# Graph layer of a GNN and mixture-of-experts block: two bins of nodes to a PSUM bank, one look a turn, row lists by fourteens

## What is computed

```
y = layernorm(x)
w_full = einsum('rb,bdo->rdo', w_comp, weight)          # 16 relations out of 8 bases
msg = einsum('nd,rdo->rno', y, w_full)[etypes, src] * edge_weight
x = x + relu(segment_sum(msg, dst) + h_bias + y @ loop_weight)
x = x + expert_layer(layernorm(x))
```

## Time and profile before

| | us |
|---|---|
| median of three runs (3833.6 to 3851.45) | 3844.34 |
| profiled execution, its own time | 3843.4 |
| its span, first to last instruction | 3841.7 |
| graph layer: first gather issued | 215.1 |
| last gather issued | 3008.9 |
| last multiplication of a turn starts | 3101.3 |

### The profile page before, as it was taken

One profiled execution on the slowest core, in us unless ns is written; L12 is line 12 of the kernel. 1 busy time (PEld: TensorE's weight loads), 2 busy tenths in 40 slices (PEclk: granted clock), 3 DMA queues, 4 the chain that ended last, 5 costly groups with the idle time before them and its releaser, 6 DMA issues. The chain is left out here.

```text
span 3841.7 us, 44188 instructions
## 1 busy us (share of the span) xinstructions
PE 2433.4 (63%) x11555; PEld 1907.4 (50%) x11556; DVE 942.2 (25%) x2185; ACT 682.4 (18%) x1839; POOL 1874.2 (49%) x2177
## 2 busy tenths in 40 slices
PE   3544454554655655666666666767767756999976
PEld 1422332433543443454454455555556536888865
DVE  4611111121102112121111111112112246333336
ACT  0510000000011111111111122212222211222234
POOL 0466666566546546555545445345544201444433
PEclk9866676776877877888878877888788878999998
DMA  3442333233223223222222223222222242112135
GB/s 117 146 135 85 88 92 88 75 92 97 73 75 90 78 74 94 77 82 80 78 76 78 78 76 90 66 68 78 83 83 64 52 144 93 63 63 63 61 123 189
DMA packets 144937, 337.27 MB, mean 88 GB/s; under 512 B 36515, under 2 KB 52163, under 8 KB 144740
## 3 DMA queue, kind: packets, MB, share of 16 engines
q0 software_dynamic: 89392, 245.59, 21.9%
q1 hardware_dynamic: 34239, 51.42, 3.9%
q10 hardware_dynamic: 21252, 39.56, 3.0%
HBM read 289.22 MB, written 50.42 MB: 88 GB/s over the span
## 5 line engine op out<-in xcount | busy, mean ns | idle before, releaser
L1176 PE MATMUL psW<-rows,S 128*128 x3920 | 1192.7, 459 | 878.2 <-issue 590.9
L994 POOL DMA_INDIRECT rows<-feat,idx x1568 | 1489.9, 950 | 479.6 <-issue 460.5
L1176 PEld LDWEIGHTS psW<-rows,S 128*128 128x128 f32 x3920 | 850.2, 228 | 1215.1 <-issue 1095.4
L1076 DVE TENSOR_TENSOR S<-psHere,coefS 128x896 f32<-128x896 f32 x280 | 303.8, 1091 | 2227.8 <-PE psW L1176 1244.3
L1235 ACT COPY z<-psW 128x256 f32<-128x256 f32 x392 | 145.6, 371 | 2064.1 <-PE psW L1176 1080.2
L977 POOL COPY idx<-srcT 128x7 int32 (+1 forms) x224 | 43.6, 195 | 783.9 <-PE psW L1176 616.4
L1139 PE MATMUL psG<-wb,zT 128*128 128x256 f32 (+1 forms) x1600 | 357.9, 382 | 0.0
L1139 PEld LDWEIGHTS psG<-wb,zT 128*128 128x128 f32 (+1 forms) x1600 | 304.1, 190 | 47.5 <-issue 1.0
L1126 PE MATMUL psZ<-ident,z 128*128 128x128 f32 x784 | 152.5, 352 | 197.1 <-ACT z L1235 91.2
L1126 PEld LDWEIGHTS psZ<-ident,z 128*128 128x128 f32 x784 | 114.8, 180 | 236.0 <-issue 184.5
L1562 PE MATMUL psH<-xT,w1x 128*128 128x128 f32 x1840 | 228.3, 278 | 0.2 <-DVE w1x L1604 0.2
(11 more groups left out here) (254 smaller groups left out, 1449.6 us busy)
## 6 DMA issues: line engine op xcount, KB each, us to landing
rows<-feat,idx POOLq DMA_INDIRECT x1568
g<-expert_rows SPq DMA_DIRECT2D x24, 512.0 KB, 5.8
w1s<-in_L_ffn_w SPq DMA_DIRECT2D x8, 1024.0 KB, 10.7
w2s<-in_L_ffn_w SPq DMA_DIRECT2D x16, 512.0 KB, 10.9
featT<-fT ACTq DMA_DIRECT2D x25, 256.0 KB, 2.2
fts<-featT ACTq DMA_DIRECT2D x25, 256.0 KB
feat<-yt SPq DMA_DIRECT2D x24, 256.0 KB, 2.2
h<-in_x ACTq DMA_DIRECT2D x24, 256.0 KB
```

Of the source, the lines that this page charges most:

```text
L994: e.indirect_dma_start(rows[:, at * H:(at + 1) * H], None, d.feat, bass.IndirectOffsetOnAxis(ap=idx[:, q * GB + u:q * GB + u + 1], axis=0) ...
L1076: e.tensor_tensor(S[h][:, :].rearrange("p (s b n) -> p s b n", s=U, b=B), both[:, h * U:(h + 1) * U, :].unsqueeze(2).to_broadcast([P, U, B ...
L1176: e.matmul(psW[:, bass.ds(bank[u], H)], S[h][:, u * ZC:(u + 1) * ZC], rows[:, bass.ds(slot[u], H)], start=False, stop=True, skip_group_che ...
```

## The change

- Two bins share a bank: steps address eight half banks. ScalarE waits for the second bin of a pair, copies both to `z` with one instruction of 512 columns, and clears both with one. `wend`, the counts of `z_done` and of `cleared` go by pairs. Eight bins are in flight in place of four.
- TensorE takes a turn as a whole: one look for a tile's end, one wait for a clear place (of the turn's last bin), one for landed rows (of its last block), one for `S`, then seven multiplications. The table has 20 numbers for a turn in place of 24.
- POOL's lists are of `GB` = 14 blocks, and SyncE counts landed rows by `QB` = 7. The ring stays at 56 blocks.
- The cuts of the loop move (82, 70, 66, 62 turns), and `expand` works out the smaller tables.

```diff
-CTL = 24
+CTL = 20
 RB = 56
-GB = 7
-QB = 4
+GB = 14
+QB = 7
...
-CTL_PART = (78, 62, 70, 70)
+CTL_PART = (82, 70, 66, 62)
...
             for k in range(NB):
-                e.matmul(psW[:, k * BANK:k * BANK + H], zero[:, 0:P], zero[:, :], start=True, stop=True).then_inc(s_clear, 1)
+                e.matmul(psW[:, k * BANK:k * BANK + H], zero[:, 0:P], zero[:, :], start=True, stop=True)
+                e.matmul(psW[:, k * BANK + H:(k + 1) * BANK], zero[:, 0:P], zero[:, :], start=False, stop=True, skip_group_check=True).then_inc(s_clear, 1)
...
                         e.load(regs, ctl[part_of][:, bass.ds(i * 2 + h, 1), :])
-                        for k, (u0, n) in enumerate(PART):
-                            tile1 = e.snap(regs[AT_TILE + k], min_val=1, max_val=NT2)
-                            with e.If(e.snap(regs[AT_ENDED + k], min_val=0, max_val=1)):
-                                tile_product(tile1, TW)
...
-                            e.wait_ge(s_clear, clear)
-                            e.wait_ge(s_in, come)
-                            if k == 0:
-                                e.wait_ge(s_S, i * 2 + (first + h + 1))
-                            for u in range(u0, u0 + n):
...
+                        tile1 = e.snap(regs[AT_TILE], min_val=1, max_val=NT2)
+                        with e.If(e.snap(regs[AT_ENDED], min_val=0, max_val=1)):
+                            tile_product(tile1, TW)
...
+                        e.wait_ge(s_clear, clear)
+                        e.wait_ge(s_in, come)
+                        e.wait_ge(s_S, i * 2 + (first + h + 1))
+                        for u in range(U):
...
-                for k in range(nw):
-                    if later(t) and k == nw // 2:
+                for k in range(nw // 2):
+                    if later(t) and k == nw // 4:
                         e.wait_ge(s_tile, t)
                         columns_in(t)
                     e.wait_ge(s_P, regs[k])
-                    at = k % NB * BANK
-                    e.copy(z[:, k * H:(k + 1) * H], psW[:, at:at + H]).then_inc(s_z, 1)
-                    e.wait_ge(s_z, t * TW + k + 1)
-                    e.copy(psW[:, at:at + H], zero[:, :]).then_inc(s_clear, 1)
+                    bank = psW[:, k % NB * BANK:(k % NB + 1) * BANK]
+                    e.copy(z[:, 2 * k * H:2 * (k + 1) * H], bank).then_inc(s_z, 1)
+                    e.wait_ge(s_z, t * (TW // 2) + k + 1)
+                    e.copy(bank.rearrange("p (w o) -> p w o", w=2), zero[:, :].unsqueeze(1).to_broadcast([P, 2, H])).then_inc(s_clear, 1)
```

More of the change, by code:

```diff
@@ L70 @@
 AT_BANK, AT_SLOT = 0, U
-AT_CLEAR, AT_COME, AT_ENDED, AT_TILE = 2 * U, 2 * U + 2, 2 * U + 4, 2 * U + 6
-CTL = 24
+AT_CLEAR, AT_COME, AT_ENDED, AT_TILE = (2 * U + k for k in range(4))
+CTL = 20
+assert U <= 2 * NB - 1 and NWP % 2 == 0 and TW % 4 == 0 and WL % 4 == 0
 RB = 56
-GB = 7
-QB = 4
+GB = 14
+QB = 7
 IB = 2 * (RB // GB)
-CTL_PART = (78, 62, 70, 70)
+CTL_PART = (82, 70, 66, 62)
 assert NBLK % RB == 0 and RB % GB == 0 and RB % QB == 0 and sum(CTL_PART) == TURNS
@@ L522, in _, with second @@
             e.wait_ge(s_end, EB)
-            ch(e.tensor_tensor(wend[:, 0:NWP - 1], win_no[32:33, 0:NWP - 1], psE[32:33, 0:NWP - 1], ALU.add))
-            ch(e.memset(wend[:, NWP - 1:WPAD], STEPS))
+            def second(a):
+                return a[32:33, 0:WPAD].rearrange("o (w k) -> o w k", k=2)[:, 0:NWP // 2 - 1, 1]
+            ch(e.tensor_tensor(wend[:, 0:NWP // 2 - 1], second(win_no), second(psE), ALU.add))
+            ch(e.memset(wend[:, NWP // 2 - 1:WPAD // 2], STEPS))
         @blk.tensor
@@ L598, in expand @@
         js = sb("js", [CP, CN])
[L599 to L600 removed]
+        tw = sb("tw", [CP, 1 + CT])
+        ti = sb("ti", [CP, 1 + CT], I32)
         sno, wf, qf = (sb(n, [CP, CN]) for n in ("sno", "w_step", "qf"))
@@ L833, in at @@
                 return rows_c[:, :, k:k + n]
-            div_small(e, ch, qi[:, :], wf[:, :], qi[:, :], 1, 2)
-            ch(e.scalar_tensor_tensor(qf[:, :], qi[:, :], -float(NB), wf[:, :], ALU.mult, ALU.add))
-            ch(e.tensor_scalar(at(AT_BANK, U), turn(qf), float(BANK), None, ALU.mult))
+            div_small(e, ch, qi[:, :], wf[:, :], qi[:, :], 1, 3)
+            ch(e.scalar_tensor_tensor(qf[:, :], qi[:, :], -2.0 * NB, wf[:, :], ALU.mult, ALU.add))
+            ch(e.tensor_scalar(at(AT_BANK, U), turn(qf), float(H), None, ALU.mult))
+            div_small(e, ch, qi[:, :], wf[:, :], qi[:, :], 1, 1)
+            ch(e.tensor_scalar(at(AT_CLEAR), turn(qi)[:, :, U - 1:U], 1.0, None, ALU.add))
             div_small(e, ch, qi[:, :], js[:, :], qi[:, :], 2341, 17)
@@ L847, in _ @@
             ch(e.tensor_copy(tw[:, :], ti[:, :]))
[L848 to L854, removed]
+            now, was = tw[:, 1:1 + CT].unsqueeze(2), tw[:, 0:CT].unsqueeze(2)
+            ch.add(e.tensor_tensor(at(AT_ENDED), now, was, ALU.subtract))
+            ch.add(e.tensor_scalar(at(AT_TILE), was, 1.0, None, ALU.add))
+            ch.add(e.memset(at(AT_TILE + 1, CTL - AT_TILE - 1), 0))
+            first_of = tw[:, 0:CT].rearrange("p (t k) -> p t k", k=2)[:, :, 0:1]
+            last_of = tw[:, 1:1 + CT].rearrange("p (t k) -> p t k", k=2)[:, :, 1:2]
             ch.add(e.tensor_tensor(rows_p[:, :, 0:1], last_of, first_of, ALU.subtract))
@@ L1220, in _ @@
                 e.dma_start(to[0:1, :], zero[0:1, :]).then_inc(s_st, 16)
-            regs = [e.alloc_register(f"end{k}") for k in range(TW)]
+            regs = [e.alloc_register(f"end{k}") for k in range(TW // 2)]
             def tiles(t, nw):
-                e.load(regs, wend[0:1, bass.ds(t * TW, TW)])
+                e.load(regs, wend[0:1, bass.ds(t * (TW // 2), TW // 2)])
                 base, groups = t * NE, HC * nw // 4
@@ L1821, in gnn @@
         words = [n * CTL for n in CTL_PART]
-        own = [0, WPAD, (RB + NBLK) // GB, TURNS + 2]
+        own = [0, WPAD // 2, (RB + NBLK) // GB, TURNS + 2]
         tables = sb("tables", [97, max(n + k for n, k in zip(words, own))], I32)
```

28 lines of the change are left out of this document (12 added, 16 removed).

## The result

The changed kernel takes 3916.85 us (median of four runs, 3912.03 to 3931.96) against 3846.17 before (median of four, the three of the table and one more): **1.0195 times as long, 95% interval 1.0158 to 1.0233**. That is slower beyond the noise, though not surely by 2%. The forecast was 3764 with a range from 3650 to 3890. The profiled execution of after took 3931.96 us, 15 above its median; its span is 3930.3.

A forecast was written before the change was run, and what follows sets the result against it. With POOL's ring full, TensorE was taken to bound the graph layer, much of its idle time in its own sequencer. Late tiles -84, tile 0 0, `S` +25, places -20: -79 from 3843.4 gives 3764 us, range 3650 to 3890.

The forecast's parts named there:

- The fast turn: TensorE's turn outside slow stretches, 4.2 us: one look and a table of 20 would save 0.53 us.
- ScalarE: Copying a pair of bins would take 1.17 us in place of 1.50, hidden beside TensorE's turns.
- landed rows: Counted by seven, TensorE may see a block up to 3.75 us later, once at the start; no cost.
- tile 0: The dense first tile: savings are spent waiting for `S`, so 0 us, bounds -25 and +10.
- Lists of fourteen take part of it back: In a late tile, half a POOL stop lost by merging, at 5.4 us each: 2.7 us of the gain.
- rival (c): Fewer POOL stops leave TensorE less fast time, 5.4 us per stop lost: slower, 3900 us, chance 0.20.
- A late tile: Tiles with few blocks: shorter fast and slow turns gain 6.3 us each, 3.5 kept after the lists, -84 us.
- slow: three sequencer instructions fewer: TensorE's turns in slow stretches, 16 us each: 2.1 us saved at 0.7 us an instruction.
- waits for `S`: Faster TensorE meets VectorE's `nodes` more often: +25 us, waits for `S` up to 235 us.
- Rival (d): Nothing gained: VectorE takes over and savings stand in front of `S`, or slow stretches return them; 3835 us, chance 0.20.
- halves them, -20: TensorE's waits for a cleared place, 46.5 us, halved by eight bins in flight: -20 us.

The follow-up runs named there:

- after_lists7: The changed kernel with POOL's lists by 7 in place of 14, all else of the change kept; ratio 0.9953 to the kernel before.
- the control: The changed kernel with registers that waits compare against held at 1 or more (the clamp), as in all follow-up kernels; ratio 1.025 to the kernel before.
- after_lists4: The changed kernel with POOL's lists by 4 in place of 14; ratio 0.991 to the kernel before.
- after_ring49: The changed kernel with lists by 7 and a ring of 49 blocks in place of 56; ratio 0.9973 to the kernel before.
- before_pairs: The kernel before with the pairs of bins alone, keeping two heads, the table of 24 and lists by 7; ratio 1.0014.
- ring49_four_S: after_ring49 with TensorE's loop written out for four turns and four buffers of `S` in place of two; ratio 0.9887 to the kernel before.
- pacing: Small memsets by POOL behind each gather to space gathers out; four of them in the kernel before gave ratio 0.965.
- lists7_paced8: after_lists7 with eight small memsets by POOL behind each gather; ratio 0.8944, 3442 us where the kernel before took 3848.

## Why the prediction was wrong, step by step

- **The fast turn: right.** Predicted 0.27 us from the load and 0.26 from the head. The load went from 1616 to 1360 ns, 64 ns a register. Between loads that follow each other within 5.5 us lie 4.43 us before (mean of 137) and 3.78 after (147): 0.65 us. On the price of a register the measurement, from tables that lie in SBUF, decides against applying here the about 200 ns which the Trainium skill, "Runtime: NRT & Kernel Launch", instruction fetch mechanics, states.
- **ScalarE, landed rows, tile 0: right in size.** 586 + 589 ns for a pair; tile 0's product starts at 736.0 in place of 740.8 us, where I had 0 with bounds of -25 and +10. The reading behind tile 0 went beyond its row: the earlier trace rows puts the 14.15 us down to "issue". VectorE's row of before bears out `S`, but VectorE had no work to be slow at; it had itself stood for 23.4 us:

```profile
508.68 1.09 DVE L1076 TENSOR_TENSOR S<-psHere,coefS 128x896 f32<-128x896 f32 x1 [23.40 <-issue]
```

- **The sum has two terms that failed, and the gain is the larger.** Without the lists the forecast was 24 x 6.3 + 20 - 25 = 146 us faster; after_lists7 is 19 us faster than before (at most some 20 more without the clamp). For the lists it had 24 x 2.7 = 65 us; they cost 107 (3889 for the control, 3782 with lists by 7). So 127 us of the miss are in the gain and 42 in the lists. With the lists at their measured price and the gain as forecast, the sum is 3843 - 146 + 107 = 3804, still faster.
- **"Lists of fourteen take part of it back ... 2.7 us" a late tile: the step that failed in the lists' term.** I priced short stops that merge, 5.4 us each and half of one a tile. Short stops did become fewer (69 to 47) but their sum stayed, 292 and 299 us. The price lay where I had looked for nothing, at the tile product: POOL may not use fewer than fourteen free places there, and the products themselves took 41 us longer. By after_lists7 against the control the long stops are 100 us of it, 4 us a product in all 25 tiles. The rival (c) had the side, two of its signs (69 stops, a lower clock) and nearly the time (3900), by luck: its mechanism was this same one of merged stops. Its price also counts the 12 stops twice which the -79 already holds; by its own 5.4 us, 69 of 91 stops make 22 lost, 10 beyond the forecast's 12, and about 3818, faster than before. A smaller slip, of no weight: seven fast turns of 4.2 us are 29.4, not 29.8.
- **"A late tile ... gain 6.3 us", with "slow: three sequencer instructions fewer, 2.1 us a slow turn": the step that failed in the gain.** I took the slow stretch for TensorE's own pace, and held the tile product at its 24.7 us as if only turns could be slow. Outside the products the gain came, about 120 us. The products, which the sum had at no change, grew by 75 to 101 us (after_lists4 and after_ring49 against before_pairs), and in after, with the lists of fourteen, by 128 (708 to 836). In the turns, waits for `S` rose from 209.6 to 534.5 us (I had 235) and issue fell from 590.9 to 234.4; with `S` in advance (ring49_four_S) `S` cost 4.7 and issue was back at 614.5. What holds TensorE there is the gathers' run, not the length of its head: pacing took 3.5% off the kernel before with both heads in place. Rival (d) had the small gain, but VectorE didn't take over: it waited for TensorE's updates.
- **Places, "halves them, -20": wrong.** 144.5 us after, 72.2 in the control, 46.5 before. With the pairs and two heads it fell to 30.2 (before_pairs), nearly the 20 us less that I had. So the rise comes with the single head; the wait of 20.38 us at 685.79 shows one that ended when late updates came through.
- The range ended at 3890, since it cut off half of rival (c).

Still open: how the 3% of the wait for fourteen splits between idle places and longer crawls, why the products grew under the single head, and what in the chip lets gathers hold up other engines' instructions and updates. The runs don't tell the spacing of the gathers from the memsets between them. The transfers moved 104 GB/s in a crawl and 88 with eight memsets (480 to 510 us), but no run changed the bytes and left the rate. It was not tried either which of lists by 4, eight memsets and four buffers of `S` add up.

## What to carry to other kernels

A producer that waits for room by n places stops, as an estimate, with n/2 free ones unused (109 us by that sum here, 100 measured, of which up to 41 may have another cause); price a coarser wait by that, at the places where the consumer is away longest, and not by the number of waits that it saves. Where an engine's sequencer crawls or its semaphore updates come late, find who is working without a stop at that time, and slow that one down before shortening the victim's code: here eight memsets that put 0.18 us more between gathers gave ten per cent, and shortening TensorE's turn by 0.65 us gave 0.5%. And when a change moves work in time, don't hold the parts that it leaves alone at their old length: here the tile products, which it hardly touched, grew by 18% (708 to 836 us).

## What the runs showed of the hardware

- While indirect gathers of 128 rows of 1 KB were issued each 1.25 us, TensorE's matmul pairs came one each 1.40 us from 11 to 15 us on the earlier trace rows, and VectorE and ScalarE learned of its steps some 19 us late (684.5 for 665.4). With four memsets behind each gather, each 1.32 us, TensorE's sequencer instructions of over 0.6 us fell from 240 to 7, with eight, each 1.43, to one.
- POOL's gather doesn't suffer from it (0.95 us and a gap of 0.30 all through), its memsets do (0.70 us apart). A small memset of 0.13 us behind a gather is hidden in that gap.
- The granted clock of the layer was 0.78 before, 0.76 in the changed kernel and 0.82 (215 to 2700 us) in lists7_paced8, where TensorE had the same multiplications to do in 2,485 us and not 2,974.
